# Relative values moved by VectorE, denominators packed and inverted once, and another order at the end of an attention and feed-forward kernel

## The reference

```python
xn = layernorm(x)
q, k, v = heads(xn @ Wq.T + bq), heads(xn @ Wk.T + bk), heads(xn @ Wv.T + bv)
scores = (einsum('bhqd,bhkd->bhqk', q, k) + einsum('bhqd,qkd->bhqk', q, rel_k[idx])) / sqrt(8)
w = softmax(scores, axis=-1)
out = einsum('bhqk,bhkd->bhqd', w, v) + einsum('bhqk,qkd->bhqd', w, rel_v[idx])   # idx: clipped k - q
result = x + out @ Wo.T + bo + ffn(xn)
```

## Time and profile before

| What | Value |
|---|---|
| median of 3 runs | 478.08 us (477.27 to 479.91) |
| the profiled execution | 478.54 us |
| its span, first to last instruction | 476.7 us |
| outside the span | 1.8 us |
| PE, DVE, ACT, POOL busy | 417.7, 406.0, 416.6, 313.5 us |
| first unit of the loop to last (transposes) | 93.4 to 439.5 us |
| mean granted clock of PE | 0.97 |

### The profile page before, as it was taken

How to read it: one execution, slowest core, us unless ns; L and a number is a source line. 1 busy time by engine, 2 the same in 40 slices (tenths; PEclk the granted TensorE clock), 3 DMA queues, 4 the chain that set the end, 5 groups by cost and what they waited for, 6 DMA issues and landing times.

```text
span 476.7 us, 24894 instructions
## 1 busy us (share of the span) xinstructions
PE 417.7 (88%) x10258; PEld 337.7 (71%) x10258; DVE 406.0 (85%) x881; ACT 416.6 (87%) x806; POOL 313.5 (66%) x370
## 2 busy tenths in 40 slices
PE   0788888679999999999999999999999999999733
PEld 0345554577888887888888888888888888887622
DVE  8879766469989999999999899999999999999535
ACT  2879999469999999999999999999999999999300
POOL 6547777527574777768687768777686868775400
PEclk9989999999999999999999999999999999999955
DMA  7623745952104443424243334515242425522694
GB/s 167 221 53 111 126 89 136 168 127 69 37 27 83 72 67 71 94 43 87 55 78 73 66 67 82 96 38 92 49 82 58 71 62 93 89 55 52 119 261 130
DMA packets 159464, 43.09 MB, mean 90 GB/s; under 512 B 122256, under 2 KB 156536, under 8 KB 159224
## 3 DMA queue, kind: packets, MB, share of 16 engines
q1 hardware_dynamic: 154352, 40.45, 41.6%
q10 hardware_dynamic: 5000, 1.05, 1.3%
HBM read 21.55 MB, written 16.79 MB: 80 GB/s over the span
## 4 chain that ended last, share of the span: by engine, by line
PE 50%; issue 12%; ACT 9%; DVE 7%; DMA 1%; SPq 1%; ACTq 0%; DVEq 0%
PE ps_s L1019 10%; PE ps_s L1014 9%; PE ps_s L1116 9%; PE ps_o L1036 9%; PE ps_t L1101 7%; DVE mx L1225 5%; PE ps_r L1060 4%; ACT xr L1153 4%; ACT big L1188 4%; ACT p L1168 1%; PE ps_s L1091 1%; SPq L933 1%; DVE big L1229 1%; DMA xr<-rel_dram 1%; DMA rel_dram<-xr 1%
## 5 line engine op out<-in xcount | busy, mean ns | idle before, releaser
L860 POOL TENSOR_TENSOR big<-p,big 128x512 f16<-128x512 f32 x128 | 148.6, 1161 | 101.7 <-ACT big L1188 101.0
L1019 PE MATMUL ps_s<-by_q_room,e 96*128 96x64 f16 x2048 | 103.1, 192 | 0.0
L1014 PE MATMUL ps_s<-qbd,kst 96*128 96x128 f16 x1024 | 99.5, 219 | 3.1 <-PEq L300 2.5
L1229 DVE TENSOR_TENSOR big<-ps_y,big 128x512 f16<-128x512 f32 x128 | 88.0, 687 | 15.3 <-ACT big L1188 13.8
L1266 DVE TENSOR_REDUCE mcol<-ps_t 128x4 bf16<-128x512 bf16 x128 | 87.5, 684 | 9.0 <-PE ps_t L1101 5.3
L1225 DVE TENSOR_TENSOR mx<-s,ps_s 128x512 bf16<-128x512 bf16 x128 | 86.6, 676 | 3.2 <-ACT s L1146 2.1
L1146 ACT ACTIVATE s<-ps_s 128x512 bf16<-128x512 f32 x128 | 80.2, 627 | 6.0 <-PE ps_s L1019 5.9
L1019 PEld LDWEIGHTS ps_s<-by_q_room,e 96*128 96x128 f16 x2048 | 85.4, 97 | 0.0
L1188 ACT ACTIVATE big<-p 128x512 f16<-128x512 f32 x128 | 84.6, 661 | 0.0
L1168 ACT ACTIVATE ps_y<-ps_s 128x512 f32<-128x512 f32 x128 | 76.0, 593 | 7.5 <-PE ps_s L1116 3.1
L276 POOL COPY by_q_room<-qrel 96x256 uint32<-96x256 uint32 x128 | 78.4, 629 | 3.1 <-POOLq L300 3.1
(11 more groups left out here) (110 smaller groups left out, 523.2 us busy)
## 6 DMA issues: line engine op xcount, KB each, us to landing
rel_dram<-xr SPq DMA_DIRECT2D x32, 256.0 KB, 3.4
xr<-rel_dram SPq DMA_DIRECT2D x64, 128.0 KB, 3.7
kst<-big SPq DMA_DIRECT2D x48, 64.0 KB, 2.0
qrel<-qr_dram SPq DMA_DIRECT2D x192, 16.0 KB
qbd<-q_dram SPq DMA_DIRECT2D x192, 16.0 KB
y_dram<-big SPq DMA_DIRECT2D x4, 512.0 KB, 2.8
big<-y_dram SPq DMA_DIRECT2D x4, 512.0 KB, 6.0
out<-big SPq DMA_DIRECT2D x8, 256.0 KB, 3.4
```

The lines of the kernel that those rows point to most:

```text
L860: nc.gpsimd.tensor_tensor(probs[:, k // 8, 1, 1, k % 8, :], p32[:, k % 2, 1, :], probs[:, k // 8, 0, 1, k % 8, :], ALU.subtract).then_inc( ...
L1014: nc.tensor.matmul(bank[:, P * g:P * g + P], kst[:, g, S * k + P * kh:S * k + P * kh + P], rhs, start=(g == 0), stop=False, skip_group_che ...
L1019: ins = nc.tensor.matmul(bank.rearrange("p (h q j) -> p h q j", q=Q0, j=J)[:, :, q, :], e4[:, first:first + P], rhs.rearrange("p (h j) -> ...
L1229: nc.vector.tensor_tensor(probs[:, k // 8, 1, 0, k % 8, :], ps_y[:, :], probs[:, k // 8, 0, 0, k % 8, :], ALU.subtract).then_inc(lo0_ready, 1)
```

## The change

- move_relative goes from ACT to DVE, as a tensor_copy of the same tile. In iteration k it stands behind maximum(k + 1), in front of own_heads. The waits are the same.
- For blocks 0 to 12 the denominators are taken otherwise: SP loads one of the 8 equal rows of each query from rel_dram into a small tile packed (128x32; 4 DMAs, load_packed), DVE inverts it in one instruction (reciprocals_of, iteration 23 of the block's count), SP saves the result to rec_dram (1 DMA) and loads it back with each value repeated for the 8 components (4 DMAs, load_reciprocals). POOL's normalize waits for that load. The 4 pieces per block on DVE fall away.
- In the last pass the 8 relative parts of block 14 go two at a time into iterations 9 to 12, and its two moves into iterations 11 and 13.
- After the loop: block 15 is moved by ACT (move_last), and loaded in halves, half of the groups from SP's queue and half from ACT's (load_last); SP has another order; DVE finishes blocks 14 and 15 in halves (finish_half), and project waits for both halves of a block.

The diff, cut to its core:

```diff
+    PACKED = BG * NQB - 3
         def relative_of(qb, k, first):
+            if qb == NQB - 1 and k in (first - 2, first):
+                return qb, 0, (k - first + 2) // 2
             for bg in range(BG):
                 for half in range(2):
                     at = first + 8 * bg + 4 * half
-                    if k == at % UNITS and (at < UNITS or unit(qb, -1)):
-                        return qb - at // UNITS, bg, half
+                    own = qb - at // UNITS
+                    if k == at % UNITS and own >= 0 and (own, bg) != (NQB - 1, 0):
+                        return own, bg, half
+        def load_last(eng, half, groups):
+            m = BG * NQB - 1
+            eng.wait_ge(rel_out[half], 16 * (m + 1))
+            for g in groups:
+                src = rel_dram[m, g, half].rearrange("j (y d) (h n) -> (d h) j y n", d=HD, h=HH)
+                eng.dma_start(land[32 * g:32 * g + 32, m % 2, 4 * half:4 * half + 4, :, :], src).then_inc(last_in[half], 16)
             def normalize(m):
-                pool.wait_ge(rrden_ready, 4 * (m + 1))
+                if m < PACKED:
+                    pool.wait_ge(rec_in[m % 2], 16 * G * (m // 2 + 1))
+                else:
+                    pool.wait_ge(rrden_ready, 4)
+            def load_packed(m):
+                for half in range(2):
+                    sp.wait_ge(rel_out[half], 16 * (m + 1))
+                if m > 1:
+                    sp.wait_ge(rec_ready, m - 1)
+                for g in range(G):
+                    src = rel_dram[m, g, :, :, HD, :].rearrange("i j (h n) -> h (i j) n", h=HH)
+                    sp.dma_start(packed[32 * g:32 * g + 32, m % 2, 0, :], src).then_inc(packed_in[m % 2], 16)
+            def save_reciprocals(m):
+                sp.wait_ge(rec_ready, m + 1)
+                sp.dma_start(rec_dram[m].rearrange("g h (x n) -> (g h x) n", n=QN), packed[:, m % 2, 1, :]).then_inc(rec_out[m % 2], 16)
+            def load_reciprocals(m):
+                sp.wait_ge(rec_out[m % 2], 16 * (m // 2 + 1))
+                if m > 1:
+                    sp.wait_ge(att_ready, m - 1)
+                for g in range(G):
+                    src = rec_dram[m, g].rearrange("h (o n) -> o h n", o=1).to_broadcast([HD, HH, 8 * QN])
+                    sp.dma_start(rrden[32 * g:32 * g + 32, m % 2, :], src).then_inc(rec_in[m % 2], 16)
             def body(qb, last):          # SP
                     if su >= 3:
                         save_relative(su - 3, 1)
+                    if su >= 4:
+                        load_reciprocals(su - 4)
                     sp.wait_ge(by_q_ready, 8 * su)
                     load_rel_queries(sp, v, qb, bg)
+                    if su >= 3:
+                        load_packed(su - 3)
...
                     load_queries(sp, v, qb, bg)
...
                         load_relative(su - 3)
+                        save_reciprocals(su - 3)
                     if su >= 2:
                         save_relative(su - 2, 0)
...
             save_relative(last - 2, 1)
+            load_reciprocals(last - 3)
             load_relative(last - 2)
             save_relative(last - 1, 0)
             save_relative(last - 1, 1)
             load_rest(0)
+            load_rest(1)
             load_relative(last - 1)
-            load_rest(1)
-            save_relative(last, 0)
             load_rest(2)
             load_rest(3)
-            save_relative(last, 1)
-            save_out(0, 0)
-            save_out(0, 1)
-            load_relative(last)
-            for m in range(1, len(OUT_PARTS)):
+            for half in range(2):
+                save_relative(last, half)
+            sp.wait_ge(att_ready, last - 1)
+            for half in range(2):
+                load_last(sp, half, range(0, 2))
+            for m in range(len(OUT_PARTS)):
...
             def relative_step(qb, k):    # PE
+                if qb == NQB - 1 and 9 <= k < 13:
+                    relative(qb, 0, 2 * (k - 9))
+                    relative(qb, 0, 2 * (k - 9) + 1)
...
-                wait(pe, last_ready, (0, 1 + bg)[qh])
+                wait(pe, last_ready, (0, 2 + 2 * bg)[qh])
...
-            relative(NQB - 1, 0, len(REL_PARTS) - 1)
...
-            move_relative(NQB - 1, 0, 1)     # ACT, after the loop
-            move_relative(NQB - 1, 1, 0)
-            move_relative(NQB - 1, 1, 1)
+            for half in range(2):
+                move_last(half)
+            act.wait_ge(att_ready, BG * NQB - 2)
+            for half in range(2):
+                load_last(act, half, range(2, 4))
...
+            def move_relative(qb, bg, half):     # DVE; ACT's is gone
+                done = 2 * (BG * qb + bg) + half + 1
+                dve.wait_ge(rel_ready, done)
+                wait(dve, rel_out[half], 16 * (BG * qb + bg))
+                nc.vector.tensor_copy(rT[:, half, :].rearrange("p (h s b) -> p h s b", h=H, b=8),
+                                      ps_r[:, :].rearrange("p (s b h) -> p h s b", s=4, h=H)).then_inc(rel_moved, 1)
+            def reciprocals_of(m):
+                dve.wait_ge(packed_in[m % 2], 16 * G * (m // 2 + 1))
+                wait(dve, rec_out[m % 2], 16 * (m // 2))
+                nc.vector.reciprocal(packed[:, m % 2, 1, :], packed[:, m % 2, 0, :]).then_inc(rec_ready, 1)
             def body(qb, last):          # DVE
...
                         maximum(qb + 1, 0)
+                    rel = relative_of(qb, k, 13)
+                    if rel:
+                        move_relative(*rel)
                     if unit(qb, k - 3):
                         own_heads(*unit(qb, k - 3))
-                    for piece in range(4):
-                        m = block_at(qb, k, 25 + piece)
-                        if m is not None:
-                            denominators(m, piece)
+                    m = block_at(qb, k, 23)
+                    if m is not None and m < PACKED:
+                        reciprocals_of(m)
...
-            add_rest(0)
             own_heads(NQB - 1, UNITS - 1)
             sum_heads(NQB - 1, UNITS - 1)
-            finish_block(BG * NQB - 2)
+            add_rest(0)
+            for half in range(2):
+                finish_half(BG * NQB - 2, half)
             add_rest(1)
-            finish_block(BG * NQB - 1)
+            finish_half(BG * NQB - 1, 0)
             add_rest(2)
+            finish_half(BG * NQB - 1, 1)
             add_rest(3)
```

More of the change, by code:

```diff
@@ L73, in layer_kernel @@
         rel_dram = nc.dram_tensor("rel_dram", (BG * NQB, G, 2, 4, 32, P), F32, kind="Internal").ap()
+        rec_dram = nc.dram_tensor("rec_dram", (BG * NQB, G, HH, 8 * QN), F32, kind="Internal").ap()
         identf = sb("identf", [P, P], F32)
@@ L165, in layer_kernel @@
         mcol = sb("mcol", [P, 2, G], BF16)
+        packed = sb("packed", [P, 2, 2, QN], F32)
         own = sb("own", [P, 2, D], F32)
@@ L771, in build_main @@
     s0, p32, rT, land, rrden, wo_sb = v["s0"], v["p32"], v["rT"], v["land"], v["rrden"], v["wo_sb"]
+    packed, rec_dram = v["packed"], v["rec_dram"]
     attT, mx, mcol, rel_dram = v["attT"], v["mx"], v["mcol"], v["rel_dram"]
@@ L809, in build_main @@
         rrden_ready, att_hi_added, att_lo_added, att_ready = sem("rrden_ready"), sem("att_hi_added"), sem("att_lo_added"), sem("att_ready")
+        last_in = [sem(f"last_in{i}") for i in range(2)]
+        packed_in, rec_out, rec_in = ([sem(f"{name}{i}") for i in range(2)] for name in ("packed_in", "rec_out", "rec_in"))
+        rec_ready = sem("rec_ready")
         last_hi_added, last_lo_added, last_ready = sem("last_hi_added"), sem("last_lo_added"), sem("last_ready")
@@ L1070, in relative_step @@
                         part = k + UNITS * back - (9 + 8 * bg)
+                        if qb - back == NQB - 1:
+                            continue
                         if 0 <= part < len(REL_PARTS) and not (back and isinstance(qb, int) and qb == 0):
@@ L1146, in copy_half, with move_last @@
                 nc.scalar.activation(s0[:, :], ps_s[:, k % 2, 0, :], ACT.Copy).then_inc(half_copied, 1)
[L1148 to L1152, removed]
+            def move_last(half):
+                act.wait_ge(rel_ready, 4 * NQB - 1 + half)
+                act.wait_ge(rel_out[half], 16 * (BG * NQB - 1))
                 nc.scalar.activation(rT[:, half, :].rearrange("p (h s b) -> p h s b", h=H, b=8),
@@ L1194, in body @@
                         exponentials(*unit(qb, k - 1))
-                    rel = relative_of(qb, k, 13)
-                    if rel:
-                        move_relative(*rel)
                     if unit(qb, k - 1):
@@ L1248, in sum_heads @@
                                         X_AXIS, ALU.add).then_inc(out_summed, 1)
+            def reciprocals_of(m):
+                dve.wait_ge(packed_in[m % 2], 16 * G * (m // 2 + 1))
+                wait(dve, rec_out[m % 2], 16 * (m // 2))
+                nc.vector.reciprocal(packed[:, m % 2, 1, :], packed[:, m % 2, 0, :]).then_inc(rec_ready, 1)
             def denominators(m, piece):
```

(20 more changed lines are left out.)

## The result

The changed kernel takes 532.38 us (median of 4 runs, 529.29 to 533.99) against 477.88 us (4 runs, 477.27 to 479.91): the ratio is 1.1124, 95% interval 1.1058 to 1.1191. It is slower by 54.5 us, where 484.4 us and a range up to 492 were predicted. The direction was right, the size was not.

The account below looks back on a forecast made before the run. PE was taken to bind an ordinary unit, ACT and VectorE a hair behind. Terms +12.2 + 2.5 + 1.1 - 9.5 = +6.3 on 478.54 us gave 484.8, or 484.4 as a median; range 469.5 to 492.

Parts of the forecast that it names:

- The stall behind VectorE's move: In the loop, PE's relative part waits 0.81 us for VectorE's move against 0.39 today, 29 times: 12.2 us lost.
- The packing of block 14: In units 9 to 12 of the last pass, PE does two relative parts each: +1.1 us.
- SP's queue: In the loop, new small transfers and a later save delay the queries' loads in some 4 of 12 blocks: +2.5 us.
- the room: Between the end of the queries' issue on SP and their use: 6.2 us in one block, 4.5 in another.
- the landing: Time from issue to arrival of the queries' loads: not shown, taken as 2.0 us, with half as the other end.
- POOL's waits for the relative queries: POOL's pair copies run about 1.5 us behind their turn; low parts are used two units later: cost nothing.
- Rival B: Queries come late in every block of the loop: 501 us at the worst, 494 for half; chance 0.09.
- The direction: Whole kernel: slower, with a chance of 0.67, against 0.21 for faster and 0.12 for the same.
- The tail: After the loop, block 14 loaded earlier and block 15 finished in halves: gain 9.5 us, bounds 5 and 11.5.
- The last projection: At the kernel's end, kept at 3.75 us at half clock; at full clock the sum would be 1.7 us lower.
- The reciprocals' removal: In the loop, 52 pieces of 534 ns leave VectorE; PE's 2.6 us covers them, so removal is worth nothing.

Follow-up runs that it names:

- the kernel with both loads moved: Changed kernel with SP's reciprocal loads moved to the end of the previous block's turn and packed loads behind the queries' loads: 485.23 us, ratio 1.0151.
- the last two experiments: Changed kernel without packed path, PE's parts deferred, pieces spread over units 26, 27, 28, 30: 470.49 us; that kernel with block 14's last-pass parts and moves rescheduled: 472.75 us.

## Why the prediction was right in its direction and wrong in its size

- **The stall behind VectorE's move** held: predicted 29 x 0.42 = 12.2 us. Measured 29 waits, units of 3.43 against 2.99 with ACT: 29 x 0.44 = 12.8 us. Shown by the waits' disappearance in the kernel with ACT's moves, and by the two kernels that change only the place on VectorE or the place on PE.
- **The packing of block 14:** predicted +1.1. The last six intervals of the kernel with both loads moved sum to 18.1 us against 16.4 before, 0.9 of it the dearer moves: +0.8.
- **SP's queue** is the step that failed: predicted 2.5 us, upper end 20, measured 47.6 us, the difference of the two loops (407.9 and 360.3 us) that differ only in SP's order. It failed in three places. First, the new loads were priced at 0.34 us each after the queries' rows, with 0.6 as an outer bound; they take 0.62 and 0.66. The trace of before had a dearer row too, the output weights' loads (4 KB each, 0.63 us), and I didn't take it. That is 2.6 us more per block, and lifts the lateness (1.1 us from the later save and 5.4 from the new loads) above the room (6.2 or 4.5 us, less the landing of 1.5) in every block, not in 4 of 12; PE's waits are 28.6 us. Second, a late block was priced at its wait alone, and the clock's fall behind most of the stops costs 15.1 us more. Third, POOL's waits for the relative queries stood at nothing, and they cost PE 3.9 us. The range up to 492 also left out its own upper end of 20 for this term, which alone gives 502; even that was less than half of what came. The landing was within my bounds.
- **Rival B** named this mechanism and its sign, at most 501 us, with a chance of 0.09. Its price used the same 0.34 and the bare wait.
- **The direction** was not luck: with the queries in time the kernel is still slower, 485.23 us, where the sum without its SP term says 481.9, and the tail makes the difference.
- **The tail:** predicted -9.5, bounds 5 and 11.5, measured -5.7 (37.2 to 31.5 us). The order of steps was right. Block 14's load beside the loads of the rest held SP for 6.99 us (500.56 to 507.55), and two loads of the rest stand behind it, so block 15's saves went out at 510.53, later than its moves at 507.63 and 509.40; and DVE takes 5.1 us from the first half's data to last_ready, since add_rest(2) and both halves stand in a row, where I had 2.4:

```profile
500.56 6.99 SPq L954 DMA_DIRECT2D xr<-rel_dram  x4
...
510.53 2.20 SPq L943 DMA_DIRECT2D rel_dram<-xr  x2
...
519.74 0.96 DVE L1326 RECIPROCAL xr<-xr 128x64 f32<-128x64 f32 x2 [2.56 <-DMA xr<-rel_dram]
...
524.41 0.38 DVE L1377 TENSOR_TENSOR attT<-attT,xr 128x128 f32<-128x128 f32 x1
524.90 3.56 PE L1147 MATMUL ps_s<-xr,attT 128*128 128x128 f32 x16 [6.75 <-issue]
```

- **The last projection** ran at a granted clock of 0.55, near the lower level again, 3.56 us against the 3.75 that I kept. By the Trainium skill ("TensorE: Matmul & The Clock Gate", part 1), activity releases the throttle; the gap of 6.75 us in front of it gave none, and the row and the rule agree.
- **The reciprocals' removal** is worth nothing in the units with ACT's moves, as predicted: 2.99 us with the pieces and without. Beside VectorE's moves it is worth up to 0.25 us per block.

The sum in measured terms: 12.8 + 0.8 + 47.6 - 5.7 = 55.5 us; the spans of the two profiled executions differ by 55.2.

## What to carry to other kernels

A DMA queue is an engine: price each new issue by a measured row, carry the dearest of the rows that might fit into the forecast (here 0.63 us beside 0.30), and give each transfer behind it a due time; here 5.4 us of new issues in front of twelve urgent loads cost 47.6 us, nearly four times the stall behind the moves that the timeline of the engines showed at first sight. Work handed to a less busy engine is only free at the place in that engine's order where its reader isn't waiting yet; moving it by two instructions of VectorE was worth the whole 0.44 us in the units without a reciprocal piece in front, and putting its reader off by one unit was worth at least as much. A wait that doesn't fit in its slack costs more than its length once PE's clock falls behind it: here 28.6 us of waits brought 15.1 us more.

## What the runs showed of the hardware beyond that

- The issue time on SP didn't follow the bytes: 0.30 us for a queries' load of 16 KB, 0.34 for the save of the reciprocals (16 KB), 0.62 for a packed load (4 KB) and 0.66 for a reciprocals' load (32 KB).
- Behind a stop of 3.76 us PE was granted 0.55 of its clock over the next 3.78 us and 73 instructions, and behind stops of 1.57, 1.70 and 2.06 us all of it; the loop has a mean granted clock of 0.96 where it was 1.00. The kernel before has no such stops in its loop.
- Four loads of 128 KB beside the 512 KB loads of the rest held SP for 4.1 us in the kernel before, 7.0 in the changed one and 2.7 and 5.8 in the last two experiments, where they took 2.1 to 3.5 in the loop of the kernel before. What sets this is not shown.
